# The end of the message stage of a fused graph and mixture-of-experts kernel: placing rows earlier, the last part contracted in two halves, identity products in TensorE's pauses

## The reference

```python
# message layer: 20000 edges, 64 paths; a row is 16 segments of 32 elements
x1 = layernorm(x)[src].reshape(-1, 16, 32)
x2 = edge_attr.reshape(-1, 16, 32)
contrib = path_coeffs[None, :, None] * x1[:, i1, :] * x2[:, i2, :]
edge_out = zeros.at[:, i3, :].add(contrib)      # per edge, sum into 16 segments
x = x + zeros(625, 512).at[dst].add(edge_out)   # edges are sorted by dst
# expert layer: h = layernorm(x)
shared = sum over 2 shared experts of (silu(h @ Wg) * (h @ Wu)) @ Wd
gate   = softmax(h @ Wr), best 6 of 64, normalised
routed = sum over 64 experts of the same FFN times gate[:, e]
x = x + shared + routed + h
```

## Time and profile before

| | |
|---|---|
| median of 3 runs | 1064.9 us (1064.45 to 1065.46) |
| profiled execution, own time | 1061.77 us |
| its span, first to last instruction | 1060.5 us |
| PE busy | 879.7 us (83%) |
| DVE busy | 561.8 us (53%) |
| ACT busy | 226.9 us (21%) |
| POOL busy | 350.0 us (33%) |
| mean granted clock of TensorE | 0.979 of full speed |
| DMA | 321.04 MB, mean 303 GB/s |

### The profile page before, as it was taken

One profiled execution on the slowest core, in us unless ns is written; L12 is line 12 of the kernel. 1 busy time (PEld: TensorE's weight loads), 2 busy tenths in 40 slices (PEclk: granted clock), 3 DMA queues, 4 the chain that ended last, 5 costly groups with the idle time before them and its releaser, 6 DMA issues.

```text
span 1060.5 us, 20287 instructions
## 1 busy us (share of the span) xinstructions
PE 879.7 (83%) x7194; PEld 477.5 (45%) x7195; DVE 561.8 (53%) x1321; ACT 226.9 (21%) x580; POOL 350.0 (33%) x390
## 2 busy tenths in 40 slices
PE   0267677677767768899999999999997989999987
PEld 0033334333334334575454644646445445454455
DVE  6499999999999999575211111111110211211116
ACT  1032222233232221331211111111210211212100
POOL 3654434534533520023323232232322331332120
PEclk9999999999999999999999999999998999999999
DMA  7857657657656644767999999999999999999918
GB/s 223 330 204 236 216 196 246 203 198 245 203 200 235 218 180 160 284 224 255 384 392 399 395 394 401 390 396 388 395 394 403 385 395 393 395 388 397 380 59 331
DMA packets 70370, 321.04 MB, mean 303 GB/s; under 512 B 12908, under 2 KB 13061, under 8 KB 48344
## 3 DMA queue, kind: packets, MB, share of 16 engines
q1 hardware_dynamic: 48050, 260.82, 64.6%
q0 software_dynamic: 21248, 56.55, 16.3%
q10 hardware_dynamic: 934, 1.80, 0.6%
HBM read 308.55 MB, written 13.62 MB: 304 GB/s over the span
## 4 chain that ended last, share of the span: by engine, by line
PE 61%; DVE 16%; issue 9%; DVEq 8%; DMA 3%; POOL 1%; SPq 1%; ACT 0%; POOLq 0%; ACTq 0%
PE ps L1249 21%; DVE big L611 12%; PE ps L1295 11%; PE ps L630 9%; PE ps L875 5%; DVEq L609 5%; PE ps L1193 4%; PE ps L902 3%; DVEq L602 3%; PE ps L1242 2%; DMA big<-y_d 2%; PE ps L1269 1%; PE ps L1267 1%; POOL big L339 1%; PE ps L1289 1%
## 5 line engine op out<-in xcount | busy, mean ns | idle before, releaser
L611 DVE TENSOR_TENSOR big<-big 128x512 f32 (+1 forms) x640 | 384.2, 674 | 15.1 <-DMA big<-xn_d,idx 15.1
L630 PE MATMUL ps<-big,mixed 128*32 128x256 f32 x2512 | 166.5, 404 | 135.2 <-DVE big L611 135.2
L1249 PE MATMUL ps<-big 128*64 128x512 f32 x1024 | 239.1, 610 | 13.5 <-issue 13.5
L339 POOL DMA_INDIRECT big<-xn_d,idx x157 | 170.2, 1084 | 196.2 <-DVE big L611 147.1
L1154 POOL DMA_INDIRECT big<-h_d,idx x64 | 63.0, 984 | 359.2 <-issue 274.9
L630 PEld LDWEIGHTS ps<-big,mixed 128*32 128x32 f32 x2512 | 78.2, 114 | 227.6 <-DVE big L611 155.4
L1259 DVE TENSOR_TENSOR mixed<-big,ps 128x256 f32<-128x256 f32 x64 | 26.9, 421 | 268.8 <-ACT big L1256 268.4
L1249 PEld LDWEIGHTS ps<-big 128*64 128x64 f32 x1024 | 69.2, 139 | 138.4 <-issue 132.7
L1295 PE MATMUL ps<-big,mixed 128*64 128x256 f32 x1024 | 124.6, 385 | 0.1
L1210 POOL DMA_INDIRECT y_d<-big,sia x74 | 75.3, 1017 | 123.0 <-DVE big L1308 102.9
L1295 PEld LDWEIGHTS ps<-big,mixed 128*64 128x64 f32 x1024 | 68.0, 137 | 35.5 <-issue 3.1
(11 more groups left out here) (213 smaller groups left out, 670.6 us busy)
## 6 DMA issues: line engine op xcount, KB each, us to landing
big<-in_L_ffn_Wg SPq DMA_DIRECT2D x64, 1024.0 KB, 16.2
big<-in_L_ffn_Wu SPq DMA_DIRECT2D x64, 1024.0 KB, 20.7
big<-in_L_ffn_Wd SPq DMA_DIRECT2D x64, 1024.0 KB, 15.9
big<-in_edge_attr SPq DMA_DIRECT2D x39, 1024.0 KB, 6.1
big<-y_d SPq DMA_DIRECT2D x10, 768.0 KB, 12.1
big<-xn_d,idx POOLq DMA_INDIRECT x157
big<-in_L_ffn_sWg SPq DMA_DIRECT2D x2, 1024.0 KB, 10.8
big<-in_L_ffn_sWu SPq DMA_DIRECT2D x2, 1024.0 KB, 13.1
```

What stands on the lines that cost most here:

```text
L339: pool.indirect_dma_start(xs[s][:, c, :], None, xn_d[:, :], bass.IndirectOffsetOnAxis(ap=table[:, c0 + c:c0 + c + 1], axis=0)).then_inc(x_ ...
L611: ins = dve.tensor_tensor(pr[k % 2][:, 0:chunks, EXT * p:EXT * (p + 1)], xs[s][:, 0:chunks, ds(o1, EXT)], es[s][:, 0:chunks, ds(o2, EXT)], ...
L630: ins = pe.matmul(edge_bank(k // 2)[WIN * h:WIN * (h + 1), h0:h0 + HP * EXT], onehot[s][:, CW * h + r, :], pr[k % 2][:, CW * h + r, :], st ...
L1249: ins = pe.matmul(bank(k2)[TA * h:TA * (h + 1), :].rearrange("p (w f) -> p w f", w=2), xgT[k2][:, k, 0:TA], gu[:, :, k, W * h:W * (h + 1)] ...
```

## The change

It has three parts, all in the message stage.

1. `place_rows` of group `t` is called behind part 6 of the loop and no longer behind part 7, for all ten groups.
2. For the last group alone, the last part (7) is contracted by a new function in two halves of 128 columns: half 0 when DVE has done four of the part's eight paths (new semaphore `half_ok`), then `select` of the third bank, then half 1. So `select` moves ahead of half 1.
3. `stay_warm(n)` issues `n` matmuls of the identity with itself, 128 columns, into columns of the bank of the third part, which nothing reads any more: three ahead of the last `turn`, four ahead of the last `select`, two ahead of the last five `put`s. They wait for nothing.

```diff
--- before.py
+++ after.py
@@ -561,6 +561,7 @@
     nmax = nc.values_load(ntab[0:1, 0:1], min_val=0, max_val=MAXJ)
 
     part_used = sem("part_used")
+    half_ok = sem("half_ok")
     oh_ab, oh_ok = sem("oh_ab"), sem("oh_ok")
     pl_ab, place_ok = sem("pl_ab"), sem("place_ok")
     ev_ok, tp_ok, evt_ok, sel_ok, sum_ok = (sem(n) for n in ("ev_ok", "tp_ok", "evt_ok", "sel_ok", "sum_ok"))
@@ -610,6 +611,8 @@
                 o2 = dve.snap(rg[2 * p + 1], min_val=0, max_val=D - EXT)
                 ins = dve.tensor_tensor(pr[k % 2][:, 0:chunks, EXT * p:EXT * (p + 1)],
                                         xs[s][:, 0:chunks, ds(o1, EXT)], es[s][:, 0:chunks, ds(o2, EXT)], ALU.mult)
+                if p == HP // 2 - 1 and k == SUB - 1 and at(t, NG - 1):
+                    ins.then_inc(half_ok, 1)
                 if p == HP - 1:
                     ins.then_inc(part_ok, 1)
                 if k <= EC // PER and (p % PER == PER - 1 or p == HP - 1):
@@ -631,6 +634,26 @@
                                 onehot[s][:, CW * h + r, :], pr[k % 2][:, CW * h + r, :], start=r == 0,
                                 stop=r == min(CW, chunks - CW * h) - 1)
         ins.then_inc(part_used, 1)
+
+    def contract_half(t, s, half):
+
+        k, w = SUB - 1, HP // 2 * EXT
+        if half == 0:
+            pe.wait_ge(half_ok, 1)
+        else:
+            pe.wait_ge(part_ok, SUB * t + k + 1)
+        for r in range(CW):
+            for h in range(QW):
+                ins = pe.matmul(edge_bank(k // 2)[WIN * h:WIN * (h + 1), HP * EXT + w * half:HP * EXT + w * (half + 1)],
+                                onehot[s][:, CW * h + r, :], pr[k % 2][:, CW * h + r, w * half:w * (half + 1)],
+                                start=r == 0, stop=r == CW - 1)
+        if half == 1:
+            ins.then_inc(part_used, 1)
+
+    def stay_warm(n):
+
+        for _ in range(n):
+            pe.matmul(edge_bank(PARTS - 2)[:, 0:P], ident[:, :], ident[:, :], start=True, stop=True)
 
     def evict(t, qq):
 
@@ -700,13 +723,19 @@
         chunks = EC if t else EC0
         products(t, s, 16 * QW * (t // 2 + 1), 16 * EC * (t // 2) + 16 * (EC if s else EC0), chunks)
         for k in range(SUB):
-            contract(t, s, k, chunks)
+            last = t == NG - 1 and k == SUB - 1
+            if last:
+                contract_half(t, s, 0)
+            else:
+                contract(t, s, k, chunks)
             q = PARTS * t + k // 2 - 1
             if q >= 0 and k % 2 == 0:
                 turn(q // PARTS, q % PARTS)
                 evict_turned(q // PARTS, q % PARTS)
             if q >= 0 and k % 2 == 1:
                 select(q // PARTS, q % PARTS)
+            if last:
+                contract_half(t, s, 1)
             if k % 2 == 1:
                 evict(t, k // 2)
             if t > 0 and k == 1:
@@ -716,12 +745,15 @@
             if t + 1 < NG and 2 <= k < 6:
                 one_hots(t + 1, 1 - s, lambda c: wdst[:, EC * (t + 1) + c:EC * (t + 1) + c + 1],
                          CW * (k - 2), CW * (k - 1))
-            if k == SUB - 1:
+            if k == SUB - 2:
                 place_rows(t, nrow[:, t:t + 1])
+    stay_warm(3)
     turn(NG - 1, PARTS - 1)
     evict_turned(NG - 1, PARTS - 1)
+    stay_warm(4)
     select(NG - 1, PARTS - 1)
     evict_sums(NG - 1)
+    stay_warm(2)
     put(NG - 1, range(NB), stop=True)
 
     gu_in = [sem(f"gu_in{k}") for k in range(4)]
```

## The result

The changed kernel is slower: 1071.4 us as median of six runs (1070.31 to 1071.8), beside 1065.0 us for the kernel before in six runs (1064.25 to 1065.9). The ratio is 1.0058, interval 1.0043 to 1.0074. The forecast was 1063.4 us, range 1062.3 to 1065.6. The profiled execution of the changed kernel took 1071.78 us, 10.0 more than that of before (1061.77); its span is 1070.3 us against 1060.5, its mean granted clock 0.973 against 0.979.

The account below looks back on a forecast made before the run. DMA transfer bounds 494 to 1012 us, starting when routing and first experts allow. Off the median 1064.9: 0.10 halves + 0.54 placing rows - 0.07 four products + 0.98 clock = 1.55 us, giving 1063.4 us; range 1062.3 to 1065.6 (8 in 10).

Parts of the forecast that it names:

- The step that failed: Behind the last puts: keep_clock starts at 437.31 after 0.67 us of idle PE; the transposes wait for DVE until 442.63.
- the second rival: Low clock moves into routing behind PE's longer pause, costing up to 1.7 us: 1065.05 or 1066.0 us; chance 0.13.
- The halves: Last group's last contraction: two halves of 1.15 us each, ending at 427.96 and not 428.06, 0.10 us won.
- the best end named: Halves at 0.11 us a step: the last contraction ends at 427.76, 0.30 us better.
- Placing rows and four products: Chain from turn to select: moving place_rows wins 0.54 us, four identity products ahead of select cost 0.07.
- The clock, 0.98 us: Last puts: PE nearly without pause, so full clock, about 4.5 us and not 6.25; 0.98 us won.
- the first rival: The clock gives nothing, the low stretch being one execution's; only the chain's 0.57 us is won: 1064.3 us; chance 0.23.
- One microsecond for one: A microsecond won at the end of the message stage is one microsecond of the whole, and no more.

Follow-up runs that it names:

- e1: The kernel before with place_rows behind part 6 alone: 1061.24 us, ratio 1.0001.
- e3: The kernel before with the nine identity products alone (36 more PE records): 1063.03 us, ratio 1.0009.
- e10: The changed kernel with two more identity products (8 more PE instructions) ahead of the first contraction: 1065.23 us, ratio 1.0005.
- e9: The kernel before, unchanged, measured and profiled once more on the chip of the third set: 1066.48 us, ratio 1.0009.
- e2: The kernel before with only the last part in halves and the semaphore half_ok: 1060.8 us, ratio 0.9993.
- e4: The kernel before with the semaphore half_ok allocated but never used: 1061.3 us, ratio 0.9999.
- e6: The changed kernel without its nine identity products: 1063.96 us, ratio 0.9996.
- e8: The kernel before with 50 identity products (200 more PE instructions) ahead of the first contraction: 1068.03 us, ratio 1.0029.
- e11: The kernel before with 25 identity products (100 more PE instructions) ahead of the first contraction: 1072.75 us, ratio 1.0071.
- e13: The changed kernel with 8 more PE instructions ahead of the first contraction, as e10, in 12 runs on another chip: 1076.48 us, ratio 0.9997.
- e16: The changed kernel with 20 PE instructions fewer, keeping only the four identity products ahead of the last select: 1075.11 us in one run.
- e12: The changed kernel with the loads of the shared expert and expert 2 given out behind the store of H: 1087.14 us, ratio 1.021.
- e5: The changed kernel itself, run once more on another chip: 1070.85 us, ratio 1.0059.
- e7: The changed kernel with place_rows back behind part 7: 1072.08 us, ratio 1.0076.

## Why the prediction was wrong

**The step that failed** is the one that places `keep_clock`: "432.10 + 9 x 0.44 + 0.58, and 0.67 of idle as in rows 3, makes 437.31". It stands in the second rival, and the forecast rests on it too. The 0.67 us were carried along as a constant, and the sum has no term for the length of the program: every instruction counted by its duration alone. So PE was taken to be ready before DVE, and the transposes were put at 442.63, 16.55 us behind the last product; they start 22.75 behind it. The change makes PE's program 100 instructions longer (64 for the halves, 36 for nine identity products of two loads and two matmuls each), and that moved the end of a block to a place one instruction behind the jump. It costs 5.2 us against the same edits with 8 instructions more (7.54 against 2.35 of idle). The hint was in the row: 0.67 us of "issue" ahead of `keep_clock` had no releaser, and with the 6.25 us of the `put`s it was the end of a fixed 6.9 us from their start. The Trainium skill has the rule, in "Runtime: NRT & Kernel Launch", Instruction fetch mechanics: instructions are brought in blocks of 16 KiB, 256 of them, and a taken branch whose target isn't in the present two blocks stops the engine until a DMA has brought it. The traces agree (16384 B a block; the target's block starts to come at 438.1 and PE's first instruction behind the jump is at 440.7, with the idle time before it). I weighed two rules of the Trainium skill on TensorE and not this one, which would have been a reason to count where the blocks end. It names the fetch of the target; what cost here was the fetch of the block after it.

**The halves.** Forecast 1.15 us each and 0.10 won; measured 1.08 each. Half 1 ends 1.72 behind the last product against 1.98 before, 0.26 won and near the best end named, 0.30. The rule of the Trainium skill ("TensorE: Matmul & The Clock Gate", The mechanism) that a weight load overlaps a running matmul only where the row groups differ is not borne out here either: 0.81 us of loads lie within each 1.08.

**Placing rows and four products.** Together 0.47 forecast; by themselves 0.53 for 0.54 (e1) and a cost of 0.14 for all nine products (e3) where 0.07 was taken. Right in kind: ACT starts the second copy 0.03 us behind `turn`. The whole chain from the last product to the `put`s is 0.97 us shorter where 0.57 was forecast, the same in e10 against e9 (5.63 against 6.59). What I had too long is `turn` (0.72 behind half 1 and not 0.93) and the halves.

**The clock, 0.98 us.** The rows of this term were of one execution, as the first rival says. In all seven other profiles whose tail has no identity products (e1, e2, e4, e6, e8, e9, e11) the `put`s take 4.56 us. So the identity products buy nothing there that the kernel doesn't have in most executions; no run shows a gain by them. Where the low clock falls varies from one execution to the next. Behind 2.1 to 2.9 us of idle time `keep_clock` takes 5.37 us with a low clock in e1, e2, e3, e4, e8, e9 and e10, and 3.67 in e6, e13 and e16, though e13 is e10's kernel. The slow `keep_clock` is the second rival in a milder form, and not made by the change.

**One microsecond for one.** With the stop taken out, `keep_clock` starts 12.54 us behind the last product (e10) and not 14.01 (e9), the transposes 17.74 and not 19.21: 1.5 us, of which 0.96 is the chain and the rest the fetch of the jump's target, 6.91 against 7.41 from the start of the `put`s. Only the chain's part repeats. The transposes start 18.1 (before), 18.6 (e4) and 19.21 us (e9) behind the last product with the old tail, and 17.74 (e10) and 16.22 (e13) with the new, by the fetch and by where the low clock falls. In e13, with `keep_clock` at full clock, the forecast's 16.55 is met. Whether it reaches the end, the runs can't tell: 1.0005 and 0.9997, each uncertain by 0.0016, agree with 0.96 us (0.9991) and with nothing; e10's interval leaves out 0.9986, e13's doesn't.

**What stays open.** From the transposes to the end the changed kernel takes 618.6 us in both of its profiles, against 616.3 in that of before, 616.4 in e9 and 615.5 in e10. It goes mostly with the stop: four of the five profiles that have it show 618.2 to 619.1, and ten of the eleven others 615.5 to 617.5 (e12 left out). But e11, with the stop, has 616.2, and e3, without it, 618.4; so how the stop would cost these 2.3 us is not shown. With the 5.2 of the stop, less 1, they would be 6.5, beside the 6.4 us of the result.

No version was found that measurably beats the kernel before. Of the changed kernel, e10 is the better form by about 6 us.

## What to carry to other kernels

Count the instructions that an edit adds to each engine ahead of a taken jump, not only their time: 4 for each small float32 product here. Where the profile shows "issue" idle behind a jump, add or take away some ten cheap instructions far ahead of it, and see whether it moves, before the edit is judged. Before terms are taken from a profiled execution, ask what makes its own time differ from the median beside it; here the 3.1 us were named and not asked after.

## What the hardware showed that was not expected

- A block end one instruction behind a jump's target: 7.5 to 8.4 us of idle PE in four profiles (the changed kernel, e5, e7, e11), 2.1 to 2.9 in ten with the block end elsewhere, and 2.44 in e12, where it lies behind the target but no weight loads fill the DMA engines. With the block end 8 instructions on it splits (3.04 and 3.86 us); 20 on, `keep_clock` and the wait for the layer norm cover it.
- The block after a jump's target starts to come 3.0 to 3.6 us after PE has entered the target's block in the sixteen profiles in which weight loads fill the DMA engines (0.7 in e12, where they don't), whether PE needs it at once or not.
- The same program takes 1061.2, 1065.3, 1065.3 and 1077.1 us on four chips (31, 20, 19 and 17 runs). It goes with the arrival of PE's completions in the first half of each group, while GpSimd gathers and SP loads: in time on the first, up to 3.9 us late on the next two, up to 5.0 on the last. What makes them late was not tried.
